# Fewer words of counts, no closing matmul of a counted group, and ring places in registers, in a message-passing kernel

## What is computed

```python
S = feat[src]
for r in range(2):
    msgs = where((rel == r)[:, None], relu(relu(S @ W[r].T + b[r]) @ W[r].T + b[r]), msgs)
agg = segment_sum(msgs, dst, num_segments=n_nodes)
gates = agg @ W_ih.T + b_ih + b_hh          # i, f, g, o
hn = sigmoid(o) * tanh(sigmoid(i) * tanh(g))
x = x + relu(relu(hn @ W1.T + b1) @ W2.T + b2) @ W3.T + b3
```

## Time and profile before

| | |
|---|---|
| median of three runs | 1219.66 us (1217.96 to 1224.33) |
| the profiled execution | 1206.18 us, its span 1204.4 us |
| mean granted TensorE clock in it | 0.81 of full speed |
| busy: PE, POOL, DVE, ACT | 784.6, 470.4, 429.3, 352.2 us |

### The profile page before, as it was taken

One profiled execution on the slowest core, in us unless ns is written; L12 is line 12 of the kernel. 1 busy time (PEld: TensorE's weight loads), 2 busy tenths in 40 slices (PEclk: granted clock), 3 DMA queues, 4 the chain that ended last, 5 costly groups with the idle time before them and its releaser, 6 DMA issues.

```text
span 1204.4 us, 14814 instructions
## 1 busy us (share of the span) xinstructions
PE 784.6 (65%) x2859; PEld 422.7 (35%) x2859; DVE 429.3 (36%) x1285; ACT 352.2 (29%) x724; POOL 470.4 (39%) x518
## 2 busy tenths in 40 slices
PE   5898417355455746637667994478276679866895
PEld 4667103122222312313333552135133435423564
DVE  6687406243433524524421313012211411320446
ACT  2443529052342612514313320112022113112141
POOL 3000450644434254171365556370724462564200
PEclk9999558676767967767879997698688879877998
DMA  6212220312212122030143222130312231233303
GB/s 197 70 60 72 78 80 1 88 57 62 62 49 71 33 83 62 19 102 22 55 143 109 71 78 85 48 105 5 105 31 70 59 87 48 74 88 66 36 2 107
DMA packets 47768, 82.45 MB, mean 68 GB/s; under 512 B 14287, under 2 KB 31712, under 8 KB 47712
## 3 DMA queue, kind: packets, MB, share of 16 engines
q0 software_dynamic: 23040, 62.95, 19.0%
q1 hardware_dynamic: 22272, 15.15, 4.1%
q10 hardware_dynamic: 2400, 3.67, 0.9%
HBM read 71.72 MB, written 9.75 MB: 68 GB/s over the span
## 4 chain that ended last, share of the span: by engine, by line
PE 44%; issue 25%; DVE 9%; another core or an unknown queue 8%; DVEq 7%; ACT 4%; ACTq 2%; DMA 0%; PEldq 0%
PE BIG L841 14%; PE AG L947 8%; PE BIG L985 6%; PE SM L892 4%; DVE oh_key L1326 3%; PE BIG L802 3%; DVEq L1326 3%; PE SM L1016 2%; PE AG L813 2%; PE SM L813 2%; DVEq L1337 1%; PE BIG L783 1%; ACTq L682 1%; ACT oh_row L682 1%
## 5 line engine op out<-in xcount | busy, mean ns | idle before, releaser
L598 POOL DMA_INDIRECT ring<-message_table,rows x480 | 460.9, 960 | 668.3 <-PE AG L947 398.9
L985 PE MATMUL BIG<-oh_key,oh_row 128*128 x572 | 159.1, 403 | 179.2 <-issue 122.3
L1326 DVE TENSOR_SCALAR oh_key<-iota,lists 128x400 f16 x572 | 156.5, 328 | 254.4 <-issue 177.0
L947 PE MATMUL AG<-ring,onehot 128*128 x564 | 158.6, 409 | 57.3 <-issue 39.6
L985 PEld LDWEIGHTS BIG<-oh_key,oh_row 128*128 x572 | 61.2, 107 | 270.1 <-issue 254.0
L682 ACT ACTIVATE oh_row<-iota,lists 128x128 f32 x320 | 104.2, 390 | 110.8 <-issue 64.3
L841 PE MATMUL BIG<-fT,half_a 128*128 128x512 f32 (+1 forms) x192 | 91.7, 634 | 61.6 <-ACT fT L748 49.0
L1354 DVE TENSOR_TENSOR onehot<-dst,iota_b 128x512 f16 x141 | 59.3, 425 | 192.7 <-PE AG L947 112.3
L947 PEld LDWEIGHTS AG<-ring,onehot 128*128 x564 | 64.9, 115 | 143.7 <-issue 118.5
L841 PE MATMUL BIG<-half_b,half_a 128*128 128x512 f32 (+2 forms) x200 | 85.4, 584 | 36.4 <-ACT late L730 32.5
L892 PE MATMUL SM<-half_b,late 128*128 128x256 f32 x400 | 92.9, 385 | 0.9 <-ACT late L753 0.9
(11 more groups left out here) (191 smaller groups left out, 661.6 us busy)
## 6 DMA issues: line engine op xcount, KB each, us to landing
ring<-message_table,rows POOLq DMA_INDIRECT x480
message_table<-late SPq DMA_DIRECT2D x10, 512.0 KB, 3.5
out<-X SPq DMA_DIRECT2D x24, 128.0 KB
X<-in_x SPq DMA_DIRECT2D x5, 512.0 KB, 6.4
half_a<-in_f ACTq DMA_DIRECT2D x1, 1024.0 KB
half_b<-in_f ACTq DMA_DIRECT2D x1, 1024.0 KB
message_table<-late SPq DMA_DIRECT2D x2, 384.0 KB, 2.9
half_a<-in_w_ih_t ACTq DMA_DIRECT2D x1, 768.0 KB
```

Of the source, the lines that this page charges most:

```text
L598: nc.gpsimd.indirect_dma_start(ring[:, to * W:(to + 1) * W], None, table, bass.IndirectOffsetOnAxis(ap=rows4[:, k:k + 1], axis=0)).then_in ...
L947: mm = nc.tensor.matmul(AG[b % 2][:, :], tile_of(hots, j), rows[:, 2 * j * W:2 * (j + 1) * W].bitcast(F16), start=not more and j == 0, sto ...
L985: mm = nc.tensor.matmul(b[:, 0:GC], rows[:, 2 * j * P:2 * (j + 1) * P].bitcast(F16), keys[:, 2 * j * GC:2 * (j + 1) * GC].bitcast(F16), st ...
L1326: last = nc.vector.tensor_scalar(ones_of[:, j, :], iota16[:, :], key4[:, j:j + 1], float(-g * GC), ALU.subtract, ALU.is_equal)
```

## The change

- A word holds three counts: three groups (22 words) or three blocks (9 words, loaded at blocks 0, 3, 6 to 24). The halves of a block are no longer two counts: one count is split in two by a shift, after the first visit. Block HOT counts its first quad as one more, so it is split 5 and 5.
- The closing matmul of a counted group is gone. ACT keeps a register of the counting visits so far, and waits until the semaphore hot_used[1], which the last matmul of each visit raises, has reached it. `filled()` numbers big_full without the groups. ACT makes the rows of the next word ahead of the last evacuation of this one.
- PE keeps the places of this and the next quad (and row) in registers and moves them on behind a visit.
- In blocks 0 to HOT no first visit is made; one matmul over zeros, 128x512, opens the bank. Visits are 137 instead of 141.
- `released` starts at RQ - 1; the dense pieces come one bundle later; `make_plan` packs with the function `packed`; one memset on POOL is gone.

The constants, the numbers of big_full, and the order of the dense pieces:

```diff
-    PACK = 3 if HG % 3 == 0 else 2
+    PACK = 3
+    TRIO = 3
...
+        def filled(*key):
+            n = at[("big",) + key]
+            return n + 1 - sum(1 for item in big_items[:n] if item[0] == "counts")
...
-                    if b and 1 <= i <= PIECES:
-                        bundle.append(("dense", (b - 1, i - 1)))
-                    if b and i == PIECES + 2:
+                    if b and 2 <= i < PIECES + 2:
+                        bundle.append(("dense", (b - 1, i - 2)))
+                    if b and i == PIECES + 3:
```

On ACT, `rows_of` and the copy of the counts:

```diff
-                more = (word >> 8) + (word & (BYTE - 1))
+                parts = [act.snap((word >> (8 * k)) & (BYTE - 1), min_val=0, max_val=BYTE - 1) for k in range(PACK)]
+                for k, m in enumerate(parts):
+                    parts_of[w * PACK + k] = m
+                more = sum(parts[1:], parts[0])
...
-                    if s % PACK == 1 and s + 1 < HG:
+                    if (s + 1) % PACK == 0 and s + 1 < HG:
                         rows_of((s + 1) // PACK)
...
-                    b = big("counts", s)
+                    b = BIG[at[("big", "counts", s)] % 4]
+                    act.reg_mov(visits_done, act.snap(visits_done, min_val=1, max_val=HG * QP + HG + KR) + parts_of[s] + 1)
+                    act.wait_ge(hot_used[1], visits_done)
+                    act.sem_inc(rows_seen, 1)
```

On PE, the start and `visit`:

```diff
-            pe.sem_inc(released, RQ)
+            pe.sem_inc(released, RQ - 1)
...
-                if more or b == 0:
-                    pe.wait_ge(landed, quads_in if more else 1)
-                quad = pe.snap(quads_in, min_val=2, max_val=NB * QP)
-                at_quad = pe.snap(((quad if more else quad - 1) % RQ) * (8 * W), min_val=0, max_val=(RQ - 1) * 8 * W)
+                if more:
+                    pe.wait_ge(landed, quads_in)
+                at_quad = pe.snap(next_quad if more else this_quad, min_val=0, max_val=(RQ - 1) * 8 * W,
+                                  guaranteed_mod_val=0, out_of_modulus=8 * W)
...
+                    if j == 1 and meanwhile:
+                        meanwhile()
...
                 if more:
                     pe.reg_add(quads_in, quads_in, 1)
+                    pe.reg_mov(this_quad, at_quad)
+                    pe.reg_mov(next_quad, (at_quad + 8 * W) % (RQ * 8 * W))
```

On PE, `segment`:

```diff
-                    blocks_of[b] = pe.value_load(plan[0:1, 7, b:b + 1], min_val=0, max_val=BYTE * BYTE - 1)
+                    if b % TRIO == 0:
+                        blocks_of[b // TRIO] = pe.value_load(plan[0:1, 7, b // TRIO:b // TRIO + 1], min_val=0,
+                                                             max_val=BYTE ** TRIO - 1)
...
-                    visit(b, False)
-                more = blocks_of[b] & (BYTE - 1) if rest else blocks_of[b] >> 8
+
+                    def parts():
+                        m = pe.snap((blocks_of[b // TRIO] >> (8 * (b % TRIO))) & (BYTE - 1), min_val=0, max_val=BYTE - 1)
+                        parts_of[b, True] = pe.snap(m >> 1, min_val=0, max_val=BYTE - 1)
+                        parts_of[b, False] = pe.snap((m + 1) >> 1, min_val=0, max_val=BYTE - 1)
+                    if b > HOT:
+                        visit(b, False, parts)
+                    else:
+                        nc.tensor.matmul(AG[b % 2][:, :], zeros[:, 0:P], zeros[:, 0:1].broadcast_to([P, W]), start=True, stop=False,
+                                         skip_group_check=True)
+                        parts()
+                more = parts_of[b, rest]
```

On PE, `count_visit` and `count`:

```diff
-                row = pe.snap(rows_in, min_val=2, max_val=HG * QP + 1)
-                at_rows = pe.snap(((row if more else row - 1) % RR) * (8 * P), min_val=0, max_val=(RR - 1) * 8 * P)
+                at_rows = pe.snap(next_row if more else this_row, min_val=0, max_val=(RR - 1) * 8 * P,
+                                  guaranteed_mod_val=0, out_of_modulus=8 * P)
...
+                    pe.reg_mov(this_row, at_rows)
+                    pe.reg_mov(next_row, (at_rows + 8 * P) % (RR * 8 * P))
...
-                nc.tensor.matmul(b[:, 0:2], zeros[:, 0:P], zeros[:, 0:2], start=False, stop=True,
-                                 skip_group_check=True).then_inc(big_full, 1)
```

On DVE, `segment`:

```diff
-                    visit(b, False)
-                    dve.reg_mod(col, col, 4 * QP)
-                more = blocks_of[b] & (BYTE - 1) if rest else blocks_of[b] >> 8
+                    if b > HOT:
+                        visit(b, False)
+                        dve.reg_mod(col, col, 4 * QP)
+                    m = dve.snap((blocks_of[b // TRIO] >> (8 * (b % TRIO))) & (BYTE - 1), min_val=0, max_val=BYTE - 1)
+                    parts_of[b, True] = dve.snap(m >> 1, min_val=0, max_val=BYTE - 1)
+                    parts_of[b, False] = dve.snap((m + 1) >> 1, min_val=0, max_val=BYTE - 1)
+                more = parts_of[b, rest]
```

More of the change, by code:

```diff
@@ L63, in build @@
     AB = 8
[L64 removed]
+    assert QP < BYTE and HG <= 64 and GC <= 512 and HOT <= 4
     assert D == 256 and CENTER <= 2048 and NB * P < PAD_DST and 3 * TW <= NB * P and (QP + RQ) * 4 <= TW
@@ L613, in big @@
                 n = at[("big",) + key]
-                act.wait_ge(big_full, n + 1)
+                act.wait_ge(big_full, filled(*key))
                 return BIG[n % 4]
@@ L984, in count_visit @@
                     for j in (2 * h, 2 * h + 1):
-                        mm = nc.tensor.matmul(b[:, 0:GC], rows[:, 2 * j * P:2 * (j + 1) * P].bitcast(F16), keys[:, 2 * j * GC:2 * (j + 1) * GC].bitcast(F16),
+                        mm = nc.tensor.matmul(b[:, 0:GC], rows[:, 2 * j * P:2 * (j + 1) * P].bitcast(F16),
+                                              keys[:, 2 * j * GC:2 * (j + 1) * GC].bitcast(F16),
                                               start=not more and j == 0, stop=False, skip_group_check=True)
@@ L988, in count_visit @@
                             mm.then_inc(rows_used, 1)
-                    mm.then_inc(hot_used[h], 1)
+                        if j == 1 and meanwhile:
+                            mm.then_inc(hot_used[0], 1)
+                            meanwhile()
+                    if h or not meanwhile:
+                        mm.then_inc(hot_used[h], 1)
                 pe.reg_add(hot_seen, hot_seen, 1)
@@ L1168, in make_plan, with packed @@
                 step(nc.vector.tensor_copy(plan[:, 0:6, :], pn[:, :, :]))
-                trio = pn[:, 5, 0:HG].rearrange("p (w k) -> p w k", k=PACK)
-                step(nc.vector.tensor_scalar(plan[:, 6, :], plan[:, 2, :], 1, None, ALU.arith_shift_right))
-                step(nc.vector.tensor_tensor(pn[:, 0, :], pn[:, 2, :], plan[:, 6, :], ALU.subtract))
-                step(nc.vector.scalar_tensor_tensor(plan[:, 7, :], pn[:, 0, :], float(BYTE), plan[:, 6, :], ALU.mult, ALU.add))
-                step(nc.vector.scalar_tensor_tensor(pn[:, 1, 0:HG // PACK], trio[:, :, 1], float(BYTE), trio[:, :, 0],
-                                                    ALU.mult, ALU.add))
-                nc.vector.scalar_tensor_tensor(plan[:, 1, 0:HG // PACK], trio[:, :, PACK - 1],
-                                               float(BYTE * BYTE if PACK == 3 else 0), pn[:, 1, 0:HG // PACK],
-                                               ALU.mult, ALU.add).then_inc(plan_ready, 1)
+                def packed(row, n, out):
+                    words = -(-n // 3)
+                    second, third = -(-(n - 1) // 3), -(-(n - 2) // 3)
+                    w = pn[:, 0, 0:words]
+                    step(nc.vector.tensor_copy(w, pn[:, row, 0:n:3]))
+                    step(nc.vector.scalar_tensor_tensor(w[:, 0:second], pn[:, row, 1:n:3], float(BYTE), w[:, 0:second],
+                                                        ALU.mult, ALU.add))
+                    step(nc.vector.scalar_tensor_tensor(w[:, 0:third], pn[:, row, 2:n:3], float(BYTE * BYTE), w[:, 0:third],
+                                                        ALU.mult, ALU.add))
+                    return nc.vector.tensor_copy(out[:, 0:words], w)
+                step(packed(2, NB, plan[:, 7, :]))
+                packed(5, HG, plan[:, 1, :]).then_inc(plan_ready, 1)
             def biases(*supers):
```

52 lines of the change are left out of this document (32 added, 20 removed).

## The result

The changed kernel takes 1232.74 us (median of four, 1226.71 to 1238.22), the kernel before beside it 1218.81 us: ratio 1.0126, 95% interval 1.0083 to 1.0169, some 15 us more. The forecast was 1.7 us less. The time lies in the stated range, on the side that had a chance of 0.28. The profiled execution took 1226.71 us with a span of 1224.6. It lies 6.0 us under its median, and that of before (1206.18) 12.6 us under its own, so of the 20.5 us between the two profiles only some 14 belong to the change.

What follows compares the result with a forecast made beforehand. No engine full; DVE bounds the faster counting pace, POOL's gathers the slow one, PE the gathered loops. Terms -9.5 -3.3 -2 -1 +9.1 +1 +2 +2 give -1.7: 1218.0 us, range 1202 to 1235.

Steps and rivals of the forecast that it cites:

- fewer words: Plan-word loads on all engines: 14 of 17 saved while counting at 0.68 us, -9.5; 9 in the static work, -3.3.
- One more step per visit: PE, behind a gathered visit's last matmul: one added register instruction, +3.6 while counting and +5.5 in static work, together +9.1.
- in the groups DVE covers it: PE's added step in 79 group visits: nothing, hidden by DVE's 1.35 to 1.39 us period; 11 us without cover.
- Dummy visits: Opening visits of blocks 0 to 3 go, a matmul over zeros opens the bank: -2 us, bounds 0 to -6.4.
- closings: 64 closing matmuls of counted groups on PE go: -1 us, bounds 0 and -11.4, nearly all free already.
- ACT's steps: Register instruction and event wait at each of 64 evacuations, three shifts per rows word: covered, +1 us; bounds 0 to +17.9.
- shifts: Shifts at each of 25 segments, DVE's three standing between one-hots: +2 us, 10.5 at most.
- Steps in slow stretches cost progress, not time: Added steps while POOL's gathers set the stretch's length: 3.8 us at most, +2 with ACT's and DVE's new rows.
- Case C: PE last everywhere: gathered step costs its full 16.4 us, loads give 4.3 us less; 1229.6 us, chance 0.17.
- Case B: PE's new step hides in the wait for the next one-hot, the +9.1 goes: 1208.9 us, chance 0.30.
- D: Rival: ACT becomes the bound, its added waits on the path in half the groups, +6.3: 1226.0 us, chance 0.08.
- E: Rival: saved word loads are worth nothing, a wait beneath takes each load's place: 1230.8 us, chance 0.05.

## Why the prediction was wrong

Set against the sum, in us (ratios times the kernel before's time):

| | the sum | slow kind of chip | quick kind |
|---|---|---|---|
| all but the registers | -10.8 | -0.4 (A) | -0.9 (C) |
| the registers | +9.1 | +12.6 (A, with the closings) or +15.8 (across sessions) | +6.0 (C) |
| the whole | -1.7 | +15.4 | +5.1 to +5.8 |

**The step that failed most is the savings: "fewer words", -9.5 and -3.3, and with it the terms that were to cancel each other.** Of the 17 us between forecast and result some 10 are savings that didn't come, on either kind of chip. The registers are what makes the kernel slower than the kernel before, as undoing them shows on both kinds; their price is the lesser part of the error, and on the quick kind it was put too high.

- *Fewer words, -9.5 while counting, -3.3 behind it.* The size was off: 4.9 us of the counting on chip C and 6.0 us on D, and of the whole 8.1 and 1.0 us; on the slow kind no run shows a gain at all. What failed is "so that the gap of one can't hide behind that of another". The load's gap on DVE is as costly as read (1.17 us against 0.36), but DVE isn't last in every group. On chip B, the line of the kernel before's counting matmuls:

```profile
L985 PE MATMUL BIG<-oh_key,oh_row 128*128 x572 | 126.7, 348 | 48.1 <-ACT oh_row L687 16.1 <-DVE oh_key L1326 15.5 <-issue 14.2
```

PE waited 16.1 us for ACT's rows, 15.5 for DVE's keys and 14.2 for its own steps: DVE's keys end only a third of it, so a load less on DVE can help only there. The prediction's bound of -5.2, at PE's 0.37 us, was the better value for the counting. The Trainium skill's 200 ns for a register's load ("Runtime: NRT & Kernel Launch", "Instruction fetch mechanics"; it is told of loads from HBM) gives 2.8 us by the prediction's own sum, too low for the 4.9 and 6.0 us of the counting, as the trace's 0.37 and 0.68 us had said.
- *One more step per visit.* For gathered quads the period was right to 0.01 us (1.29), and its share on the path in the counting was 4.7 us instead of 3.6. In the static work it was 0.9 us instead of 5.5 on the quick kind. **The term put at nothing failed, "in the groups DVE covers it": it costs 4.4 us of the counting.** I compared DVE's period with four matmuls of 0.84 us, and not with PE's whole turn, in which the step stands in front of the next piece of work. The two don't add: both together cost 5.2 us (280.1 against 274.9, each with large words, while 4.7 and 4.4 were measured in the kernel before).
- *Dummy visits, closings, ACT's steps, shifts: -2, -1, +1, +2.* Taken together the counting of the variant by remainder with small words is 0.6 us longer than before (279.8 against 279.2), where the sum says about 1 shorter: right within what a profile tells. In the whole they were not right: that variant is 7.2 us slower (4.9 to 9.4), and the sum has them at nothing, or +2 with the term for slow stretches. Which of them it is, or whether it is the later dense pieces or `released`, which the prediction had at nothing, no run tells: of these only the closings were put back by themselves (2.3 us less on C, not certain), and the opening visits never were.
- The counting without slow steps then adds up: -4.9 for words, +5.2 for registers, +0.6 for the rest make +0.9 (280.1 against 279.2). It must: all three are differences between the same four profiles, so this tests nothing, and that of the kernel before is of chip B, the others of C. But the whole is 5.1 to 5.8 us slower there, so 4 to 5 us lie outside the counting, and the profiles can't place them: behind the counting three of the changed kernel took 435.8, 435.9 and 440.6 us and the one of the kernel before 433.9, and the counting began at 128.9 to 131.3 us against 124.9.
- *Steps in slow stretches cost progress, not time, +2 and at most 3.8.* Undoing the registers gives 6.0 us on chip C (1.0060 to 0.9989), and 12.6 us (with the closings) to 15.8 us (0.9997 on A against 1.0126 in another session) where the steps are slow. So 7 to 10 us more hang on the same step there than on the quick kind, and the bound of 3.8 was too low. The prediction left out that a delay may move a segment's end within a burst and so lengthen the exchange behind it; the profile after looks like that at 963.46 us, but chip E shows long stalls without a longer stretch, and the gathered registers alone gave 3.5 us. How the surplus arises was not shown.
- *The rivals.* Case C had the sign, came near the time (1229.6 us) and had the place in part; its second half, loads that give 4.3 us less, came true with 4.6 in the counting. But its first half, the gathered step at its full 16.4 us, wasn't measured: on the quick kind the registers cost 6.0 us, rows' included. That its time comes near is in part luck. Case B fell: the period grew. D fell: closings back changed nothing on A. E, loads worth nothing, fell on chip C, where small words cost 8.1 us; on the slow kind it didn't fall, since small words were not slower on A.
- Open: how the 16 us divide between rows' and gathered registers where the steps are slow (the gathered ones alone gave 3.5 us there, the rows' alone weren't run on such a chip), and why small words gave 1.0041 on chip A. A median of 12 runs is good to 0.3%, and stalls of one exchange were 7 and 23 us long; that the order of exchanges and bursts made the small words look cheap was not shown.

## What to carry to other kernels

Count an engine's turn with all its register instructions, up to the point where the next work on that engine may start, before you say that another engine covers an added step. Replacing one computed value by a kept one can add an instruction: look at how the updates are packed. And a gap measured at one engine is worth at most what the other engines in the same cycle leave of it: take the smaller price first. Undo every part by itself beside the whole, on the same chip: here the prices of the parts depended on which other parts were in.

## What the runs showed of the hardware

The same kernel took 844 us on three chips and 1202 to 1222 us on two. In the first trace, of the slow kind, one column of keys took 1.40 us while POOL issued gathers, and ACT stood 31.11 us until a signal came; on the quick chip B, DVE made its one-hots at the usual pitch of 1.39 us during the same gathers. A forecast made from one chip's trace carries that chip's stalls. The changed kernel's ratio kept its sign between the two kinds (1.0126 and 1.0125 against 1.0060 to 1.0069); that of the version with large words and places by remainder didn't keep even that (0.9942 on D, 1.0028 with 0.9997 to 1.0058 on E).
